# Routing of a mixture of experts in four tile batches beside an edge stream, and one expert's weight split on GpSimd

## The reference, cut to what matters

```python
x = x + gnn(layernorm(x), edges, src, dst, W_self, W_func, W_att)   # 3125 nodes x 256, 53125 edges sorted by dst
x = x + ffn(layernorm(x)[None], router_w, w1, w2, w3)[0]

# gnn: e = leaky_relu([z[src], z[dst], w] @ W_att.T); alpha = softmax of e over the edges of one dst
#      h_new = h @ W_self.T + segment_sum(alpha * z[src], dst);  z = h @ W_func.T;  return h + relu(h_new)
# ffn (8 experts, hidden 682, top 2):
probs = softmax(flat @ router_w.T)
topk_probs, topk_idx = top_k(probs, 2)
gates = topk_probs / (topk_probs.sum(-1, keepdims=True) + 1e-9)     # scattered to [token, expert]
out = sum_e gates[:, e] * ((silu(flat @ w1[e].T) * (flat @ w3[e].T)) @ w2[e].T)
```

## Time and profile before

| what | us |
|---|---|
| median of 3 runs (lowest, highest) | 1058.42 (1057.86, 1058.95) |
| span of the profiled execution | 1057.7 |
| last logits copied (L1512), `stream_over` | 614.8, 614.9 |
| `slots_ready` tick (L1819) | 657.97 |
| first expert matmul (L1311) | 665.83 |
| busy PE, PEld, DVE, ACT, POOL | 833.1, 695.9, 619.6, 450.1, 575.1 |

### The profile page before, as it was taken

One profiled execution on the slowest core, in us unless ns is written; L12 is line 12 of the kernel. 1 busy time (PEld: TensorE's weight loads), 2 busy tenths in 40 slices (PEclk: granted clock), 3 DMA queues, 4 the chain that ended last, 5 costly groups with the idle time before them and its releaser, 6 DMA issues.

```text
span 1057.7 us, 18646 instructions
## 1 busy us (share of the span) xinstructions
PE 833.1 (79%) x4388; PEld 695.9 (66%) x4389; DVE 619.6 (59%) x2073; ACT 450.1 (43%) x1063; POOL 575.1 (54%) x556
## 2 busy tenths in 40 slices
PE   7955879865865775775777921899999999999995
PEld 6812444644654664664565711899999999999995
DVE  6524555555665666666656668456566565656553
ACT  4323243464565456456456730234344343443331
POOL 1177777777777777777775000635353544434332
PEclk9986998987887888788788955899999999999998
DMA  7775666565554545555454250452534522222221
GB/s 241 209 250 187 189 199 183 143 180 173 149 141 133 148 133 141 141 142 143 133 158 116 68 190 1 124 114 48 115 67 89 116 44 46 35 41 40 40 41 20
DMA packets 81139, 128.83 MB, mean 122 GB/s; under 512 B 21356, under 2 KB 56689, under 8 KB 80577
## 3 DMA queue, kind: packets, MB, share of 16 engines
q0 software_dynamic: 30720, 69.90, 28.6%
q1 hardware_dynamic: 43145, 51.59, 15.7%
q10 hardware_dynamic: 7200, 6.56, 1.8%
HBM read 106.86 MB, written 17.86 MB: 118 GB/s over the span
## 4 chain that ended last, share of the span: by engine, by line
PE 54%; DMA 11%; issue 11%; POOL 10%; DVE 9%; DVEq 2%; POOLq 0%; ACT 0%; SPq 0%; ACTq 0%
PE bank L1311 17%; PE bank L1237 13%; POOL early L780 8%; DMA early<-ztab,early 8%; PE bank L1350 6%; PE bank L1201 3%; PE bank L1340 3%; PE bank L1357 2%; PE bank L1083 2%; PE bank L1168 2%; PE bank L1165 2%; PE bank L1099 1%; DMA out_rows<-late,slot_rows 1%; DVE acc L1607 1%; POOL out_rows L824 1%
## 5 line engine op out<-in xcount | busy, mean ns | idle before, releaser
L780 POOL DMA_INDIRECT early<-ztab,early x416 | 396.4, 953 | 173.2 <-issue 170.5
L1311 PE MATMUL bank<-split_w,operands 128*128 x1344 | 237.7, 326 | 2.8 <-DVE operands L1839 1.4
L1237 PE MATMUL bank<-early,W 128*128 128x258 f32 x832 | 232.4, 432 | 6.5 <-DVE W L1584 6.0
L1311 PEld LDWEIGHTS bank<-split_w,operands 128*128 128x128 f32 x1344 | 213.6, 190 | 9.4 <-issue 7.4
L1237 PEld LDWEIGHTS bank<-early,W 128*128 128x128 f32 x832 | 172.0, 216 | 55.0 <-issue 23.6
L831 POOL DMA_INDIRECT xg<-ttab,slot_rows x56 | 57.6, 1028 | 230.4 <-DVE late L1866 180.2
L982 ACT ACTIVATE W<-early 128x128 f32<-128x128 f32 x208 | 91.0, 484 | 128.1 <-PE bank L1237 124.7
L1201 PE MATMUL bank<-ident,early 128*16 128x128 f32 x104 | 24.2, 380 | 138.7 <-DVE early L1567 138.7
L1201 PEld LDWEIGHTS bank<-ident,early 128*16 128x16 f32 x104 | 10.3, 120 | 150.6 <-DVE early L1567 148.0
L824 POOL DMA_INDIRECT out_rows<-late,slot_rows x56 | 88.9, 1588 | 34.0 <-issue 15.6
L1052 ACT ACTIVATE late<-bank 128x384 f32<-128x384 f32 x56 | 27.5, 491 | 187.6 <-PE bank L1311 187.6
(11 more groups left out here) (232 smaller groups left out, 1320.8 us busy)
## 6 DMA issues: line engine op xcount, KB each, us to landing
W<-in_wt SPq DMA_DIRECT2D x26, 512.0 KB, 4.8
W<-in_experts SPq DMA_DIRECT2D x40, 266.5 KB, 2.8
early<-ztab,early POOLq DMA_INDIRECT x416, 2.8
W<-in_experts SPq DMA_DIRECT2D x3, 2132.0 KB, 11.7
early<-in_x SPq DMA_DIRECT2D x26, 128.0 KB, 2.2
early<-ztab SPq DMA_DIRECT2D x25, 128.0 KB
early<-late SPq DMA_DIRECT2D x25, 128.0 KB
out_rows<-early ACTq DMA_DIRECT2D x25, 128.0 KB, 1.9
```

Of the source, the lines that this page charges most:

```text
L780: nc.gpsimd.indirect_dma_start(out=zg[:, k * KG + c, :], out_offset=None, in_=ztab, in_offset=bass.IndirectOffsetOnAxis(ap=src_here[:, k / ...
L1237: last = mm(ps[2 + k // 2 % 2][:, 0:ZR], prob_hot[:, k % 3, c * P:(c + 1) * P], zg[:, k * KG + c, :], start=(k % 2 == 0 and c == 0), stop= ...
L1311: last = mm(bank[:, 0:n], x[:, (k % 2 * KC + c) * P:(k % 2 * KC + c + 1) * P], split_w[:, bass.ds(at + (part + w + c * H), n)], start=(i = ...
```

## The change

The 25 tiles are routed in four batches, tiles 0-6, 7-13, 14-19 and 20-24. The first three are stages of the stream's turns: a batch that ends before tile `hi` does its steps in turns 4hi + 30 to 4hi + 38 (58 to 67, 86 to 95 and 110 to 118), each as the last stage of the turn. The fourth follows the last turn. A token's place is a cell (expert, 128-block of its rank) and a row in it; one-hot matrices are fp16, 100 cells by 256 rows, one pair for each (tile, choice), in chunks of three. They accumulate in PSUM bank 1 over all four batches, and two small matmuls move cells to slots. Prefix sums over tiles are DVE adds of 8 elements. SP stores the gates in two parts before its waits for the experts' weights. Expert 0's high and low parts are both made by POOL, right after the last weighted sum; expert 1's high parts by ACT in turn 1 of the experts. Engines start the experts on `expert_ready`. Some constants are made by DVE before the stream.

```diff
+ROUTES = ((0, 7), (7, 14), (14, 20), (20, TILES))
+RB = max(hi - lo for lo, hi in ROUTES)
+ROUTE_RING = 2
+CHUNK = 3
+CHUNKS_OF = [-(-2 * (hi - lo) // CHUNK) for lo, hi in ROUTES]
...
+        def split_first(pool):
+            pool.wait_ge(experts_in[0], 16)
+            for piece in range(2):
+                a, b = PIECES[piece]
+                nc.gpsimd.tensor_tensor(split(0, 0, piece), raw(0, piece), ones[:, 0:1].to_broadcast([P, b - a]), ALU.mult)\
+                    .then_inc(first_hi, 1)
+            for piece in range(2):
+                pool.wait_ge(first_hi, 1 + piece)
+                pool.sem_inc(hi_split, 1)
+                nc.gpsimd.tensor_tensor(split(0, 1, piece), raw(0, piece), split(0, 0, piece).bitcast(fp32), ALU.subtract)\
+                    .then_inc(lo_split[piece], 1)
...
+        def early_route(t):
+            for b, (lo, hi) in enumerate(ROUTES[:-1]):
+                i = t - BATCH * (hi - 1)
+                if 0 <= i < 5 + CHUNKS_OF[b]:
+                    return b, i
+            return None, None
...
+            early = ROUTES[-1][0]
+            gates_out = ttab[:, C:TR].rearrange("(t p) e -> p t e", p=P)
+            sp.wait_ge(gates_ready, len(ROUTES) - 1)
+            sp.dma_start(gates_out[:, 0:early, :], gates[:, 0:early, :]).then_inc(gates_stored, 16)
+            sp.wait_ge(gates_ready, len(ROUTES))
+            sp.dma_start(gates_out[:, early:TILES, :], gates[:, early:TILES, :]).then_inc(gates_stored, 16)
...
+                pool.wait_ge(sums_psum, GROUPS)
+                split_first(pool)
...
             act.wait_ge(finish_over, 1)
-            for e in range(2):
-                act.wait_ge(raw_in, e + 1)
-                split_hi(act, e)
-            act.wait_ge(slots_ready, 1)
+            act.wait_ge(expert_ready, 1)
+            def second_hi(t, k, r):
+                if isinstance(t, int) and t == 1:
+                    act.wait_ge(raw_in, 2)
+                    split_hi(act, 1)
...
+                for b, (lo, hi) in enumerate(ROUTES[:-1]):
+                    if in_stream and j == hi + 2:
+                        pe.wait_ge(choice_ready, 3 * b + 3)
...
+            def rank_of(b):
+                lo, hi = ROUTES[b]
+                n = hi - lo
+                pe.wait_ge(choice_ready, 3 * b + 1)
+                pe.wait_ge(or_idle, min(hi + 2, TILES))
+                mm(ps[6][:, C:C + n * E], before[:, :], both[:, 0:n * E], start=True, stop=False)
+                pe.wait_ge(choice_ready, 3 * b + 2)
+                last = mm(ps[6][:, C:C + n * E], ones[:, 0:P], prefix[:, 0:n * E], start=False, stop=True)
+                if b == len(ROUTES) - 1:
+                    last = mm(ps[6][:, C + RB * E:C + (RB + 1) * E], ones[:, 0:P], prefix[:, n * E:(n + 1) * E],
+                              start=True, stop=True)
+                last.then_inc(rank_psum, 1)
...
+            def tokens_of(b, i):
+                pe.wait_ge(onehot_ready, chunk_no(b, i) + 1)
+                for q, j, at in chunk(b, i):
+                    last = mm(ps[1][0:HALF_CELLS, 0:2 * P], hot_cell[:, at, :], hot_row[:, at, :], start=(b == 0 and q == 0),
+                              stop=(b == len(ROUTES) - 1 and q == 2 * (ROUTES[b][1] - ROUTES[b][0]) - 1))
+                last.then_inc(token_psum, 1)
...
+            def slots_of():
+                pe.wait_ge(pick_ready, 2)
+                for h in range(2):
+                    last = mm(ps[2][:, 0:SLOTS], kept[0:HALF_CELLS, h, :], pick[0:HALF_CELLS, h, :], start=(h == 0),
+                              stop=(h == 1))
+                last.then_inc(token_psum, 1)
...
+            def largest_of(b, of, best, top):
+                lo, hi, n, lg, over_e, view = tiles_of(b)
+                en = exp_neg.unsqueeze(1).to_broadcast([P, n, E])
+                eq, first = cand[:, 0:RB * E], per_tile[:, 4, 0:n]
+                link(v.tensor_tensor(view(eq), of, over_e(best), ALU.is_ge))
+                link(v.tensor_tensor(view(eq), view(eq), en, ALU.mult))
+                link(v.tensor_reduce(first, view(eq), AX.X, ALU.min))
+                link(v.tensor_tensor(view(top), en, over_e(first), ALU.is_equal))
+            def first_choice(b):
+                lo, hi, n, lg, over_e, view = tiles_of(b)
+                best = per_tile[:, 0, 0:n]
+                dve.wait_ge(logit_ready, hi)
+                link(v.tensor_reduce(best, lg, AX.X, ALU.max))
+                v.tensor_tensor(view(shift_l), lg, over_e(best), ALU.subtract).then_inc(shifted, 1)
+                largest_of(b, lg, best, tops[:, 0, :])
+            def second_choice(b):
+                lo, hi, n, lg, over_e, view = tiles_of(b)
+                best = per_tile[:, 1, 0:n]
+                link(v.scalar_tensor_tensor(view(rest), view(tops[:, 0, :]), MASKED, lg, ALU.mult, ALU.add))
+                link(v.tensor_reduce(best, view(rest), AX.X, ALU.max))
+                largest_of(b, view(rest), best, tops[:, 1, :])
+                if b:
+                    was = ROUTES[b - 1][1] - ROUTES[b - 1][0]
+                    v.tensor_copy(prefix[:, 0:E], prefix[:, was * E:(was + 1) * E])
+                chosen = v.tensor_tensor(both[:, 0:n * E], tops[:, 0, 0:n * E], tops[:, 1, 0:n * E], ALU.add)
+                if hi == TILES:
+                    link(chosen)
+                    chosen = v.tensor_tensor(view(both), view(both), over_e(valid[:, lo:hi]), ALU.mult)
+                chosen.then_inc(choice_ready, 1)
+                dve.wait_ge(choice_ready, 3 * b + 1)
+                for i in range(n):
+                    added = v.tensor_tensor(prefix[:, (i + 1) * E:(i + 2) * E], prefix[:, i * E:(i + 1) * E],
+                                            both[:, i * E:(i + 1) * E], ALU.add)
+                    if i < n - 1:
+                        link(added)
+                added.then_inc(choice_ready, 1)
+            def gates_of(b):
+                lo, hi, n, lg, over_e, view = tiles_of(b)
+                total, inv = per_tile[:, 2, 0:n], per_tile[:, 3, 0:n]
+                dve.wait_ge(exp_ready, b + 1)
+                link(v.tensor_reduce(total, view(ex), AX.X, ALU.add))
+                link(v.reciprocal(total, total))
+                link(v.tensor_tensor(view(shift_l), view(ex), over_e(total), ALU.mult))
+                link(v.tensor_tensor(view(rest), view(shift_l), view(both), ALU.mult))
+                link(v.tensor_reduce(inv, view(rest), AX.X, ALU.add))
+                link(v.tensor_scalar(inv, inv, 1e-9, None, ALU.add))
+                link(v.reciprocal(inv, inv))
+                v.tensor_tensor(gates[:, lo:hi, :], view(rest), over_e(inv), ALU.mult).then_inc(gates_ready, 1)
+            def ranks_of(b):
+                lo, hi, n, lg, over_e, view = tiles_of(b)
+                m = 2 * n
+                dve.wait_ge(rank_psum, b + 1)
+                if hi == TILES:
+                    link(v.scalar_tensor_tensor(count_i, ps[6][:, C + RB * E:C + (RB + 1) * E], float(P - 1), cell_base,
+                                                ALU.add, ALU.subtract))
+                v.tensor_tensor(cand[:, 0:m * E].rearrange("p (c x) -> p c x", c=2), tops[:, :, 0:n * E],
+                                ps[6][:, C:C + n * E].unsqueeze(1).to_broadcast([P, 2, n * E]), ALU.mult).then_inc(choice_ready, 1)
+                dve.wait_ge(choice_ready, 3 * b + 3)
+                link(v.tensor_reduce(rank_f[:, 0:m], cand[:, 0:m * E].rearrange("p (q e) -> p q e", e=E), AX.X, ALU.add))
+                link(v.tensor_copy(rank_i[:, 0:m], rank_f[:, 0:m]))
+                v.tensor_scalar(row_i[:, 0:m], rank_i[:, 0:m], 2 * P - 1, None, ALU.bitwise_and)
+                link(v.tensor_scalar(cell_i[:, 0:m], rank_i[:, 0:m], 8, None, ALU.logical_shift_right))
...
+            def one_hots(b, i):
+                if chunk_no(b, i) >= ROUTE_RING:
+                    dve.wait_ge(token_psum, chunk_no(b, i) - ROUTE_RING + 1)
+                for q, j, at in chunk(b, i):
+                    v.tensor_scalar(hot_row[:, at, :], iota_h, row_of[:, q:q + 1], None, ALU.is_equal)
+                    last = v.tensor_scalar(hot_cell[:, at, :], iota_h[:, 0:HALF_CELLS], cell_f[:, q:q + 1], token_id[:, j:j + 1],
+                                           ALU.is_equal, ALU.mult)
+                last.then_inc(onehot_ready, 1)
+            def route_rest(first):
+                for b in range(first, len(ROUTES)):
+                    first_choice(b)
+                    second_choice(b)
+                    gates_of(b)
+                    ranks_of(b)
+                    for i in range(CHUNKS_OF[b]):
+                        one_hots(b, i)
+                v.tensor_scalar(dump_p, node_id[:, 0:1], float(DUMP - HALF_ID), None, ALU.add)
+                link(v.tensor_scalar(tiles_i, count_i, 7, None, ALU.logical_shift_right))
+                link(v.tensor_copy(e8[:, 0, :], tiles_i))
+                link(v.tensor_scalar(e8[:, 0, :], e8[:, 0, :], 1.0, None, ALU.max))
...
```

(72 more changed lines are left out.)

308 lines of the change are left out of this document (144 added, 164 removed).

## The result

The changed kernel takes 1061.74 us (median of 8 runs, 1060.26 to 1063.96). The kernel before took 1058.08 us beside it (8 runs, 1057.15 to 1059.69). The ratio is 1.003, with a 95% interval of 1.0018 to 1.0042: slower by 0.3%, a small amount that can be measured. I had predicted 1060. The profiled span is 1061.0 us, and the mean granted clock 0.895 of full speed (0.893 before).

The account below looks back on a forecast made before the run. Four stages with four limits: gather issue, DVE then latency, DVE routing, PE. The routing's gain of 27 us goes on 11 us of batch 2 and 19 us of port waiting: span 1059.5 plus 0.7, 1060 us; range 1039 to 1066.

Parts of the forecast that it names:

- The port step: Tail: POOL's split of expert 0 makes DVE instructions with two SBUF inputs wait; all that follows is 18.6 us later.
- the one behind the 1060: Likeliest case: POOL's split holds DVE in the tail while the stream keeps its pace; 1060 us, chance 0.55.
- the prediction's own sign: Stream: a last gather later than 574 would show that the stream had lost its pace.
- port held and pace lost: POOL's split holds DVE and in-stream routing delays gathers, 3 us each at two places; 1066 us, chance 0.10.
- Batches 0 and 1 at 0: In the stream: 14 us of added DVE work per batch hides in idle time and slack; cost 0, at most 3 us each.
- The slack of 5 us: Stream: the first weighted sum of each cycle of four groups can come some 5 us later without delaying its gather.
- my rival: Gathers of groups 64 to 72 and 92 to 100: DVE's routing or one-hots delay them, 3 us each; chance 0.10.
- Batch 2, 11.0 us: Tail behind the last gather: 12.8 us of added DVE work, 1.8 filling idle time, makes turn 118 11.0 us later.
- Batch 3 and the slots, 16.2 us: After the tail: DVE's last routing and slot positions take 16.2 us against 43.1 before.
- From the slots on, 6.1 and up to 0.8 more: From slots ready to first expert matmul: 6.1 us instead of 7.86; the gates' store and ACT's split may add 0.8.
- Port free, 1042: Tail: POOL's split runs beside DVE without holding it; 1042 us, between 1038 and 1047, chance 0.33.
- the 0.7 us: Whole kernel: difference taken between profiled span and median time, added to the span of 1059.5.

Follow-up runs that it names:

- the run with both losses undone: Changed kernel with expert 0's split back on ACT and DVE, and DVE's ranks one turn later than PE's: 1049.44 us, ratio 0.9891.

## Why the prediction was nearly right

The time came out 1.7 us over the forecast. The port step was the right mechanism, and its size was close. But the case that came is not the one behind the 1060. By the prediction's own sign, a last gather later than 574, it is "port held and pace lost", which had a chance of 0.10 and a price of 1066; the last gather starts at 576.27. That the sum still came near 1060 is in part luck: the stream's 4.8 us, priced at nothing, and 1.8 us too many in the last stretch stand against 3.0 us that the tail, and 1.2 us that the last batch, took less than forecast.

- *Batches 0 and 1 at 0.* This is the term that was mis-sized, 0 against 4.8 us. I set DVE's 14 us against its idle time, and priced the waits that I added at nothing. The ranks' wait on PE holds DVE for 5.33 us, and behind it in order stand the next group's score steps. The slack of 5 us at the first sum of a cycle did not cover that: the gathers of groups 68 and 96 start with 2.1 and 1.9 us of extra idle time, the last gather 4.3 us late, and the last sum ends 4.8 us late. This was my rival's place and nearly its price (3 us each), but its cause was neither the amount of DVE's work nor the one-hots beside the gathers: with the ranks one turn later the same instructions leave the last gather at 571.87.
- *Batch 2, 11.0 us.* With POOL free, the tail took 26.1 us instead of 15.0: 11.1.
- *The port, 18.6 us.* POOL's four instructions took 16.7 instead of 19.0, because the first parts, with their broadcast second operand, cost 7.44 us and not 9.48. The tail shrank by 15.5 us when they went. The step let only instructions with two SBUF inputs wait; the fourth that stood, for 3.06 us, was a COPY with one (L1665).
- *Batch 3 and the slots, 16.2 us.* 15.0 to the start of the last row number. A one-hot pair of 0.28 and 0.30 us repeats every 0.41 us (priced 0.42).
- *From the slots on, 6.1 and up to 0.8 more.* 8.7. The way from the first gather to the matmul took 5.5 us against 5.2 priced (665.83 - 658.86 - 2.1 + 0.3). The rest is the store: the first gather starts 3.2 us behind the last row numbers and waits for it, where with the store out of the way it starts 1.0 us behind them (644.96 to 646.00). SP's second store, L772, stood 8.08 us at its issue behind the expert weights.
- *Sum.* Against the forecast, the stream gave +4.8, the tail -3.0, the last batch -1.2, the last stretch +1.8: +2.4 at the first matmul (670.0 against 667.6). Behind it the kernel took 0.9 us less than before, so the span is 1061.0 against 1059.5.
- *Port free, 1042.* The run without POOL's split took 1047.9, but it is not quite this case, since DVE's subtraction is back in it. Its span, 1044.6, is 3.7 us over the estimate's 1040.9; its last sum, at 603.5, was 3.6 us late, again the stream, and what the row numbers came earlier the way behind them took back. The other 2.6 us is that this median lies 3.3 us above the profiled span, where I took 0.7. Each execution's time is about 1.8 us above its own span (1046.37 for the profiled one), and the profiled one was the fastest of four. So the 0.7 us is no constant; that it is 0.7 again for the changed kernel (1061.74 - 1061.0) is chance.

## What to carry to other kernels

Before work is moved to GpSimd, list what VectorE does in that stretch by operand kind. In these traces, beside a GpSimd instruction that reads SBUF, instructions with two SBUF inputs stood until it ended, down to one element; beside one that only writes, a copy, a cast and a tensor-scalar of 8 or 12 elements did, and a copy of 8 elements stood beside a reading one too. A reduction and a tensor-scalar of one element did not stand. A step put into an in-order stream is priced by its waits and by what is queued behind them, not by its busy time: placing the consumer behind work that does not depend on the producer brought the last gather back to where it was without routing in the stream. And the same placement has to be asked about again in each stage: the order that was free in the stream cost 2.2 us in the tail.

## What the hardware showed unasked

A row gather on POOL of 0.95 us took 4.95 to 5.02 us in three kernels where it started some 0.4 to 0.5 us behind the start of DVE's two-input subtraction (4.59 us). When that gather is the first, the first matmul comes 4.4 us later behind the row numbers (12.6 against 8.2), so half a microsecond of a store can decide over four. And of two small stores issued by SP behind the same 4.3 MB of weights, the first (80 KB) took 0.49 us at its issue and the second (20 KB) 8.08 (8.15 in the run with both losses undone); from issue to landing they took 13.4 and 11.4 us.
